# Attention with probabilities and V in 32 bit: two products a strip in place of five, and all low parts of the weights on POOL

## The reference

```python
xh = x.reshape(bs, seq_len, H, d)                       # H = 16 heads, d = 16
t = jnp.einsum('bshd,hde->bshe', xh, Wqk)               # Wqk = tril @ tril.T per head
scores = jnp.einsum('bshe,bthe->bhst', t, xh) / jnp.sqrt(jnp.asarray(d, x.dtype))
attn = jax.nn.softmax(scores, axis=-1)
Vh = (x @ Wv.T + bv).reshape(bs, seq_len, H, d)
out = jnp.einsum('bhst,bthd->bshd', attn, Vh).reshape(bs, seq_len, emb_dim)
return out @ Wo.T + bo
```

## Time and profile before

| | |
|---|---|
| time, median of 3 runs | 1531.4 us (1528.1 to 1538.05) |
| the profiled execution | 1543.3 us, span 1541.6 us |
| busy over the whole span | PE 70%, PE weight loads 49%, DVE 69%, ACT 45%, POOL 32% |
| mean granted clock of TensorE | 0.83 |
| the attention stage, about 1132 to 1310 us of the span | 178 us: PE busy 151.1, DVE 134.3, ACT 136.7, POOL 101.3 |

### The profile page before, as it was taken

The page is one execution under the profiler, slowest core; times in us unless marked ns, Lnnn a source line. Parts: engine busy times, 40 slices in busy tenths (PEclk is TensorE's granted clock), DMA queues, the critical chain, the costliest instruction groups (busy, mean ns, idle before and its releaser), DMA issues. The chain is left out here.

```text
span 1541.6 us, 31533 instructions
## 1 busy us (share of the span) xinstructions
PE 1076.7 (70%) x9872; PEld 755.7 (49%) x9872; DVE 1068.9 (69%) x2356; ACT 697.0 (45%) x1392; POOL 489.6 (32%) x623
## 2 busy tenths in 40 slices
PE   4515887785199998676657867556569996479991
PEld 2212232224088885354444765334446664468881
DVE  3867999997645564565886764688768887745553
ACT  4505555553155553123425642234338887234440
POOL 0051777763145553730001100000015666232203
PEclk9557999996599999887777987678859998579996
DMA  6600000001154554312000000000013332112213
GB/s 209 205 3 11 1 1 0 1 1 43 50 151 134 162 135 152 95 42 82 1 1 1 1 1 0 0 1 0 0 43 108 115 112 70 49 46 67 64 51 119
DMA packets 47767, 89.68 MB, mean 58 GB/s; under 512 B 8353, under 2 KB 34630, under 8 KB 46790
## 3 DMA queue, kind: packets, MB, share of 16 engines
q1 hardware_dynamic: 40578, 67.98, 14.3%
q0 software_dynamic: 6912, 18.88, 4.4%
q10 hardware_dynamic: 144, 1.05, 0.2%
HBM read 71.84 MB, written 16.04 MB: 57 GB/s over the span
## 5 line engine op out<-in xcount | busy, mean ns | idle before, releaser
L909 POOL TENSOR_TENSOR scan_ch<-scan_hs,scan_ct 128x452 f32<-128x452 f32 x128 | 143.4, 1141 | 81.5 <-DVE scan_hs L1019 70.5
L932 PE MATMUL scan_py<-scan_ch,ident 128*128 128x452 f32 x256 | 130.8, 600 | 41.3 <-POOL scan_ch L909 31.6
L1019 DVE TENSOR_TENSOR_SCAN scan_hs<-scan_abar,scan_bx 128x452 f32<-128x452 f32 x128 | 132.8, 1077 | 0.9 <-ACT scan_abar L981 0.5
L458 PE MATMUL m0x_ph<-m0x_xb,m_w_hi 128*128 128x128 f16 x456 | 99.9, 221 | 0.6 <-ACT m0x_xb L1681 0.4
L459 PE MATMUL m0x_ph<-m0x_xb,m_w_hi 128*128 128x128 f16 x456 | 99.9, 221 | 0.0
L460 PE MATMUL m0x_ph<-m0x_xb,m_w_lo 128*128 128x128 f16 x456 | 99.4, 220 | 0.0
L1746 DVE TENSOR_SCALAR m3x_a<-m3x_ph,m3x_b 128x128 f32<-128x128 f32 x184 | 49.7, 343 | 68.6 <-ACT m3x_ah L1707 66.4
L932 PEld LDWEIGHTS scan_py<-scan_ch,ident 128*128 128x128 f32 x256 | 40.4, 192 | 112.7 <-POOL scan_ch L909 104.9
L981 ACT ACTIVATE scan_abar<-ssm_dt,ssm_a 128x448 f32<-128x448 f32 x128 | 80.8, 638 | 23.9 <-DVE scan_hs L1019 22.2
L1743 DVE SCALAR_TENSOR_TENSOR m0x_a<-m0x_ph,m0x_b,m0x_gate 128x128 f32<-128x128 f32 x114 | 34.7, 346 | 73.3 <-issue 39.9
L1707 ACT ACTIVATE m3x_ah<-m3x_ph,m3x_b 128x128 f16<-128x128 f32 x184 | 49.9, 382 | 64.9 <-PE m3x_ph L460 60.8
(11 more groups left out here) (679 smaller groups left out, 3816.8 us busy)
## 6 DMA issues: line engine op xcount, KB each, us to landing
mha_wbuf<-m3w SPq DMA_DIRECT2D x32, 512.0 KB, 3.7
tok_wbuf<-m0w SPq DMA_DIRECT2D x15, 768.0 KB, 5.6
m0x_b<-m0b SPq DMA_DIRECT2D x57, 128.0 KB
m_out<-m0x_yo SPq DMA_DIRECT2D x57, 128.0 KB
m3x_b<-m3b SPq DMA_DIRECT2D x23, 128.0 KB, 3.0
m_out<-m3x_yo SPq DMA_DIRECT2D x23, 128.0 KB
m_rows<-m0r_parts SPq DMA_DIRECT2D x4, 448.0 KB
m_rows<-m3r_parts SPq DMA_DIRECT2D x4, 448.0 KB
```

Of the source, the lines that this page charges most:

```text
L458: pe.matmul(out, w_hi, x_hi, start=start, stop=False)
L909: pool.tensor_tensor(ch[r][:], hs[r][:], ct[n % 2][:], ALU.mult).then_inc(weighed, 1)
L932: pe.matmul(py[c][:, 0:GT], core.ident[:], ch[u % R][:], start=n == 0, stop=n == NS - 1).then_inc(summed, 1)
L1019: dve.tensor_tensor_scan(hs[u % R][:], abar[c][:, 0:GT], bx[u % R][:], 0.0, ALU.mult, ALU.add).then_inc(scanned, 1)
```

## The change

The probabilities stay in 32 bit, in four buffers in place of two, and V is a single 32-bit tile. Both go to the products as they are: per strip one product with V and one with the block of ones, each of four heads. `round_prob`, POOL's `prob_lo`, `split_v` and the tiles for the parts are gone. weigh_v now waits for the exponentials alone, and the exponential of strip g waits for the weighing of the turn before.

The order of the work moves too. PE weighs all four strips in a row, ahead of project_v, turn_peaks and project_out. ACT's turn is: exponentials 0 and 1, take_v, take_o, exponentials 2 and 3, take_q, high of the even piece, take_qm, scale of the even piece, high and scale of the odd piece. DVE's turn begins with normalize. POOL now makes the low parts of all pieces, so ACT scales all of them, and DVE makes none.

```diff
@@ stage_attention: tiles
-        v_hi, v_lo = (st.sb(n, [L, H, 48], F16) for n in ("v_hi", "v_lo"))
-        unit = st.sb("unit", [L, 2, 48], F16)
+        v, unit = st.sb("v", [L, H, 48]), st.sb("unit", [L, 2, 48])
...
-        prob = [st.sb(f"prob{r}", [L, HG, L]) for r in two]
-        prob_hi, prob_lo = ([st.sb(f"{n}{g}", [L, HG, L], F16) for g in range(4)] for n in ("prob_hi", "prob_lo"))
+        prob = [st.sb(f"prob{g}", [L, HG, L]) for g in range(4)]
@@ POOL
-                for j in range(NB):
-                    for g in range(4):
-                        pool.wait_ge(p_high, j * 4 + (g + 1))
-                        pool.tensor_tensor(prob_lo[g][:], prob[g % 2][:], prob_hi[g][:],
-                                           ALU.subtract).then_inc(p_low, 1)
-                    mw.low_scaled(pool, 2 * j + 1, j)
+                for n in range(mw.pieces):
+                    mw.low_scaled(pool, n, n)
@@ PE, weigh_v
-                    need(pe, p_low, j * 4 + (g + 1))
+                    pe.wait_ge(exped, j * 4 + (g + 1))
...
-                    terms = ((v_hi, prob_hi), (v_lo, prob_hi), (v_hi, prob_lo), (None, prob_hi), (None, prob_lo))
-                    for n, (v, prob_part) in enumerate(terms):
+                    for n in range(2):
                         for c in range(HG):
...
-                            last = pe.matmul(pacc[rows, half * L:(half + 1) * L], w, prob_part[g][:, c, :],
-                                             start=g == 0 and n == 0, stop=g == 3 and n == len(terms) - 1)
+                            w, half = (v[:].rearrange("p h x -> p (h x)")[:, cols], k) if n == 0 else (one, KC + k)
+                            last = pe.matmul(pacc[rows, half * L:(half + 1) * L], w, prob[g][:, c, :],
+                                             start=g == 0 and n == 0, stop=g == 3 and n == 1)
@@ PE, turn
                         keep_warm(4)
-                        weigh_v(j, p, 0)
-                        weigh_v(j, p, 1)
+                        for g in range(4):
+                            weigh_v(j, p, g)
                     if ahead1:
                         project_v(j + 1)
                         turn_peaks(j + 1)
                     if behind:
                         project_out(j - 1)
-                    if now:
-                        weigh_v(j, p, 2)
-                        weigh_v(j, p, 3)
@@ ACT
-                    need(act, p_low, j * 4 + (g - 1))
-                    act.activation(prob[g % 2][:], heads(s2[g % 2]), ACT.Exp, scale=0.25).then_inc(exped, 1)
-
-                def round_prob(j, g):
-                    act.wait_ge(exped, j * 4 + (g + 1))
-
                     need(act, pv_done, j * 4 + (g - 3))
-                    act.activation(prob_hi[g][:], prob[g % 2][:], ACT.Copy).then_inc(p_high, 1)
+                    act.activation(prob[g][:], heads(s2[g % 2]), ACT.Exp, scale=0.25).then_inc(exped, 1)
@@ ACT, turn
                         take_v(j)
-                        round_prob(j, 0)
-                        round_prob(j, 1)
-                    if ahead2:
-                        take_q(j + 2)
+                    if behind:
+                        take_o(j - 1)
                     if now:
                         exponential(j, 2)
                         exponential(j, 3)
-                    if behind:
-                        take_o(j - 1)
-                    if now:
-                        round_prob(j, 2)
-                        round_prob(j, 3)
-                    if ahead1:
-                        take_qm(j + 1)
+                    if ahead2:
+                        take_q(j + 2)
                     if now:
                         if j == 0:
                             act.wait_ge(mw.ready, 2)
                         mw.high(act, 2 * j)
+                    if ahead1:
+                        take_qm(j + 1)
+                    if now:
+                        mw.scale(act, 2 * j)
                         mw.high(act, 2 * j + 1)
                         mw.scale(act, 2 * j + 1)
@@ DVE, turn
                     if behind:
-                        mw.low(dve, 2 * j - 2)
+                        normalize(j - 1)
                     if ahead1:
                         maxima(j + 1, 1 - p, 0)
                         maxima(j + 1, 1 - p, 1)
-                    if now:
-                        split_v(j)
-                    if behind:
-                        normalize(j - 1)
```

More of the change, by code:

```diff
@@ L1217, in scale @@
         act.activation(self.buf[n % self.depth][:], self.buf[n % self.depth][:], ACT.Copy, scale=WS).then_inc(self.scaled, 1)
[L1219 to L1223, removed]
     def low_scaled(self, pool, n, before):
@@ L2641, in stage_attention @@
         pacc, pt = st.ps("pacc", [128, 512]), st.ps("pt", [128, 512])
-        v_high, p_high, p_low = st.sem("v_high"), st.sem("p_high"), st.sem("p_low")
         mw = CutWeights(st, m, d, 3)
@@ L2668, in _ @@
             def _(pool):
-                for t in (v_hi, v_lo, unit):
+                for t in (v, unit):
                     pool.memset(t[:], 0.0).then_inc(ones_set, 1)
-                pool.wait_ge(ones_set, 3)
+                pool.wait_ge(ones_set, 2)
                 pool.memset(unit[:, :, 0:HD], 1.0).then_inc(ones_set, 1)
-                for j in range(NB):
-                    for g in range(4):
-                        pool.wait_ge(p_high, j * 4 + (g + 1))
-                        pool.tensor_tensor(prob_lo[g][:], prob[g % 2][:], prob_hi[g][:],
-                                           ALU.subtract).then_inc(p_low, 1)
-                    mw.low_scaled(pool, 2 * j + 1, j)
+                for n in range(mw.pieces):
+                    mw.low_scaled(pool, n, n)
             @block.tensor
@@ L2742, in weigh_v @@
                 def weigh_v(j, p, g):
-                    need(pe, p_low, j * 4 + (g + 1))
-                    if g == 0 and isinstance(j, int) and j == 0:
-                        pe.wait_ge(ones_set, 4)
+                    pe.wait_ge(exped, j * 4 + (g + 1))
+                    if g == 0 and j == 0:
+                        pe.wait_ge(ones_set, 3)
                     if g == 0:
@@ L2756, in weigh_v @@
                             cols = slice(h // 2 * 96 + odd * 32, h // 2 * 96 + odd * 32 + 32)
-                            w = one if v is None else v[:].rearrange("p h x -> p (h x)")[:, cols]
-                            half = KC + k if v is None else k
-                            last = pe.matmul(pacc[rows, half * L:(half + 1) * L], w, prob_part[g][:, c, :],
-                                             start=g == 0 and n == 0, stop=g == 3 and n == len(terms) - 1)
+                            w, half = (v[:].rearrange("p h x -> p (h x)")[:, cols], k) if n == 0 else (one, KC + k)
+                            last = pe.matmul(pacc[rows, half * L:(half + 1) * L], w, prob[g][:, c, :],
+                                             start=g == 0 and n == 0, stop=g == 3 and n == 1)
                     last.then_inc(pv_done, 1)
@@ L2827, in take_v @@
                     need(act, pv_done, j * 4)
-                    act.activation(v_hi[:, :, 0:HD], pvo[:, 0, :].rearrange("p (h e) -> p h e", e=HD), ACT.Copy,
-                                   scale=1.0 / WS).then_inc(v_high, 1)
+                    act.activation(v[:, :, 0:HD], pvo[:, 0, :].rearrange("p (h e) -> p h e", e=HD), ACT.Copy,
+                                   scale=1.0 / WS).then_inc(v_out, 1)
                 def take_qm(j):
@@ L2863, in turn @@
                         if j == 0:
-                            act.wait_ge(ones_set, 4)
+                            act.wait_ge(ones_set, 3)
                         take_v(j)
-                        round_prob(j, 0)
-                        round_prob(j, 1)
-                    if ahead2:
-                        take_q(j + 2)
+                    if behind:
+                        take_o(j - 1)
                     if now:
@@ L2897, in split_u @@
                                              ALU.add).then_inc(ac_ready, 1)
[L2899 to L2902, removed]
                 def maxima(j, p, g):
```

## The result

The changed kernel takes 1552.0 us (1547.0 to 1557.1), against 1532.2 for the kernel before in the same comparison: a ratio of 1.0121, 95% interval 1.0071 to 1.0172, some 19 us slower. The forecast was 1576. The direction held, the time lies in the range, and the size (45 us) was put more than twice too high.

A forecast was written before the change was run, and what follows sets the result against it. The prediction took a loop between four nearly full engines in the attention stage as the bound. Longer turns +37.2, the end -1.2 and clock falls +9 made +45 on 1531.4, so 1576 us; range from 1543 to 12 beyond 1588.

The forecast's parts named there:

- Stretch A: Attention turn from turn_peaks to second_pass(2), where PE waits for ACT's passes and exponentials; forecast to stay 4.71 us.
- Two loops of one length: Attention turn of 9.47 us: one loop through PE's stretches, another through ACT's scaling and POOL's low parts, tied within 0.1.
- stretch B: Attention turn from second_pass(2) to the next turn_peaks, PE's alone; forecast to grow from 4.76 to 7.24 us.
- A record streams 0.094 us: 32-bit products of weigh_v: 113 columns at two cycles each, two records an instruction, 0.19 us an instruction.
- Half overlap, 0.8 us a strip: weigh_v: a head's second record holds up the next head, eight steps of about 0.10; four strips take 3.3 us.
- the lower bound: weigh_v: the four heads overlap fully as in 16 bit, 2 x 0.19 = 0.38 us a strip.
- rival 2: weigh_v with full overlap: a strip 0.38, a turn +0.86, 1543 to 1553 us in all; chance 0.14.
- 37.2: Attention stage: fifteen intervals between turn_peaks, each 2.48 us longer, add 37.2 us.
- The clock falls in half of the turns, +9: Attention turns: PE's 1.5 us wait lowers the clock in seven of fourteen turns, 1.33 us each; ends 0 and 21.
- The end, -1.2: Last stretch, from the last turn_peaks to the reciprocal: 11.2 us in place of 12.40.
- the same sum: The whole kernel: longer turns 37.2, the end -1.2 and the clock 9, together +45 us.

The follow-up runs named there:

- experiment 8: The kernel before without the four unread products between first_pass(2) and weigh_v; the profiled execution took 1529.5 us, with turns of 9.46 to 9.48.
- experiment 2: The changed kernel with strips 2 and 3 weighed after project_out again; ratio 1.0008 to the kernel before.
- Experiment 4: The changed kernel with the two loops of weigh_v swapped, head by head; one execution, 1579.0 us beside a median of 1543.6 before.
- experiment 1: The changed kernel with ten unread products in place of four ahead of second_pass(2); ratio 1.0053 to the kernel before.
- experiment 3: The changed kernel with probabilities, V and ones as single 16-bit tiles, low parts left out; ratio 1.0117 to the kernel before.
- experiment 9: The changed kernel with ACT's even-piece scaling ahead of take_qm, no unread products before weigh_v, and normalize one turn earlier; ratio 1.0012 to the kernel before.

## Why the prediction came out as it did

- *Stretch A stays 4.71, and the removed work of ACT, DVE and POOL is worth nothing*: right. A is 4.70, and ACT waits 2.67 for turn_peaks (3 to 4 were expected). Where the prediction has PE waiting 1.5 for ACT, it waits 0.35 for DVE and 0.99 for ACT.
- *Two loops of one length, of which the change removes one*: right; experiment 8 shows the other still binding when the first is made shorter.
- *All four strips fall into stretch B*: right, and it is the cause of the loss; experiment 2 puts two of them back and is at 1.0008.
- *A record streams 0.094 us, two records an instruction*: right. Records are 260 ns, and a group of four heads' records starts every 0.097.
- *Half overlap, 0.8 us a strip*: **this is the term that failed.** It measured 0.385, the lower bound and rival 2. That rival's turn of +0.86 is the measured one, but by chance to the hundredth: its own terms, 4.76 - 0.82 + 1.6, make +0.78, or +0.89 with the 0.11 for the change of shape. I had taken it that matmuls start strictly in program order, so that one head's second record holds up the next head's first. Experiment 4 puts four such records in a row and the strips still take 1.76 us. What the runs show in its place: the four heads' column strips go on side by side, and a strip costs two products of one head, 2 x 0.19. The term cost 37.2 - 12.9 = 24 us. The Trainium skill has both rules, strict order ("TensorE: Matmul & The Clock Gate", part 3) and tiles that run independently ("TensorEngine Tiling (Array Packing)", key properties); on column strips these runs go with the second. The sixteen-bit groups could not tell them apart, since their four heads never want the same columns twice in a row.
- *The clock falls in half of the turns, +9*: right in kind, and the size is in part luck: seven falls at 1.33 were counted, and five came in the steady turns at 1.5 to 3.1 each, 10.3 in all; with turns 0 and 1 it is 12.9. They cost more where they lasted longer: the low stretch of turn 7 is 7 us long, that of turn 1 before was 3. By the Trainium skill's goals for gaps ("TensorE: Matmul & The Clock Gate", the page of part 3 above) there would have been no fall; the traces disagree, with falls where the longest wait is 0.99 us, and experiment 1 removes them by filling that wait.
- *The end, -1.2*: measured, by luck. From the last turn_peaks to the reciprocal it is 11.06, for 12.40 before. The forecast had the same 3.3 us for the four strips in it, and they did take 3.17 there, but only since the clock stood at its lower level; in experiment 1, where it did not, the stretch is 9.51, 2.9 less than before.

```profile
1312.32 0.60 PE L2744 MATMUL mha_pacc<-mha_prob,mha_v 113*32 113x113 f32 x8
...
1315.49 0.39 PE L458 MATMUL mha_pvo<-mha_wo_hi,mha_ot_hi 128*113 128x256 f16 x1
...
1317.15 1.56 DVE L2894 RECIPROCAL mha_rec<-mha_pacc 128x226 f32<-128x226 f32 x1
```

With the measured 1.69 for four strips in place of 3.3, the same sum gives 13.0 - 2.8 + 9 = +19, 1551. That this meets the measured 1552 to a microsecond is luck: the stage of the profiled execution is 24.6 longer, with 12.9 for the clock where the sum has 9, and the medians differ by 19.8.

## What to carry to other kernels

Work that an engine does while it waits for another is free, and the same work on the other side of the wait is paid in full: before moving an operation, find the one instruction at which the wait ends and ask on which side it lies. Taking work off three engines gave nothing here, as the loop went through what was left. And where TensorE idles for a microsecond each turn, price the clock too: a shorter turn with the same idle time gave no faster kernel here.

## What the runs showed that I had not expected

- Independent column strips: four heads in 32 bit take 0.19 us a product, in either order of the loops. That is what one head alone would take, by an estimate from the scan's product; one head alone was not run.
- The clock as the other half of every result: experiment 3 cut each undisturbed turn by 1.17 us and left the time at 1.0117, experiment 9 has turns 0.8 shorter than the kernel before and a ratio of 1.0012, and in it PE stayed at the lower level for 21 us while wholly busy. What starts a fall stays open: filling one wait removed them (experiment 1), the same idle time in smaller pieces brought none for 118 us (8), and a wait of 0.35 stood ahead of the longest (9).
